# A two-layer decoder on one core: norms of three layers by other engines beside a recurrence, sums placed further behind their products, maxima of a tile in two instructions

## What is computed

```
x = LN(x + spectral(x))        # layer 0 "attention"
x = LN(x + cross0(x, ctx))     # 16 heads of 16, keys of length 154
...                            # a ternary FFN, then layer 1 with three more blocks

spectral(x):
    u = LN(x) @ W_to           # real and imaginary part, 64 frequencies each
    for t in range(1024):      # serial
        s = clip(rotate(decay * s + 0.1 * u[t]), -10, 10)
    y = x + 0.1 * (s @ W_from)                     # sum, then a norm ("L=1")
    return y + 0.1 * (gelu(LN(y) @ W1 + b1) @ W2 + b2)   # sum, then a norm ("L=2")
cross0: q, k, v, softmax(q k^T) v, Wo              # sum, then a norm ("L=3")
```

## Time and profile before

| what | value |
| --- | --- |
| median of three runs | 2186.43 us |
| profiled execution, its own time | 2188.24 us |
| its span | 2186.4 us |
| recurrence, first scan to last clip | 62.5 to 602.4 us |
| first stage behind it begins | about 692.6 us |
| VectorE busy over the span | 1429.5 us (65%) |
| TensorE busy over the span | 1782.3 us (82%) |
| ScalarE busy over the span | 960.6 us (44%) |
| GpSimd busy over the span | 497.6 us (23%) |

### The profile page before, as it was taken

One profiled execution on the slowest core, in us unless ns is written; L12 is line 12 of the kernel. 1 busy time (PEld: TensorE's weight loads), 2 busy tenths in 40 slices (PEclk: granted clock), 3 DMA queues, 4 the chain that ended last, 5 costly groups with the idle time before them and its releaser, 6 DMA issues.

```text
span 2186.4 us, 34562 instructions
## 1 busy us (share of the span) xinstructions
PE 1782.3 (82%) x12969; PEld 1277.3 (58%) x12969; DVE 1429.5 (65%) x4585; ACT 960.6 (44%) x2259; POOL 497.6 (23%) x602
## 2 busy tenths in 40 slices
PE   3547666766677877999999999999888999998808
PEld 1335455654564335666666766666657999884306
DVE  4888777787822586666666566666735666663695
ACT  3524333443344743444444345445314455543762
POOL 3011112111120022333333333333302333330002
PEclk9767788878787986999999999999989999999959
DMA  5000000000000011100000000000303333310001
GB/s 153 1 1 1 1 1 1 1 1 1 1 1 1 1 39 46 38 1 1 1 1 1 1 1 1 1 1 1 122 6 88 88 83 67 86 30 0 0 0 39
DMA packets 86311, 49.81 MB, mean 23 GB/s; under 512 B 40205, under 2 KB 83905, under 8 KB 85953
## 3 DMA queue, kind: packets, MB, share of 16 engines
q1 hardware_dynamic: 79361, 47.05, 8.3%
q10 hardware_dynamic: 6784, 0.56, 0.3%
HBM read 45.50 MB, written 2.10 MB: 22 GB/s over the span
## 4 chain that ended last, share of the span: by engine, by line
PE 61%; DVE 18%; ACT 10%; POOL 3%; issue 3%; POOLq 0%; DVEq 0%; ACTq 0%
PE PS L1525 7%; PE PS L1555 6%; PE PS L1822 6%; PE PS L1542 5%; PE PS L713 3%; PE PS L1510 3%; PE PS L1500 3%; DVE sq L667 3%; DVE nx L664 3%; PE PS L719 3%; PE PS L2235 3%; PE PS L1885 2%; PE PS L1570 2%; PE PS L1841 2%; PE PS L1850 2%
## 5 line engine op out<-in xcount | busy, mean ns | idle before, releaser
L1678 POOL TENSOR_SCALAR px<-px,crl 128x128 f32<-128x128 f32 (+7 forms) x128 | 222.7, 1740 | 429.9 <-DVE crl L1650 429.9
L1593 ACT ACTIVATE px<-PS,cnm 128x128 f32<-128x128 f32 (+7 forms) x256 | 187.6, 737 | 229.4 <-DVE cnm L1635 229.4
L1635 DVE TENSOR_REDUCE cnm<-PS 128x1 f32<-128x128 f32 (+7 forms) x256 | 181.8, 751 | 73.7 <-PE PS L1530 72.0
L182 POOL TENSOR_SCALAR rstd<-mv 128x1 f32<-128x1 f32 x128 | 41.6, 325 | 796.4 <-DVE mv L161 795.7
L667 DVE TENSOR_SCALAR sq<-nx 128x4 f32<-128x4 f32 x1024 | 184.9, 181 | 35.2 <-DVE nx L664 0.2
L664 DVE TENSOR_TENSOR_SCAN nx<-sq 128x6 f32<-128x6 f32 x1024 | 175.4, 171 | 35.5 <-SPq L2302 2.3
L1542 PE MATMUL PS<-ident,px 128*128 128x128 f32 x1152 | 160.0, 278 | 5.1 <-DVE pT L1643 2.3
L1525 PE MATMUL PS<-kT,qT 64*128 64x512 f32 (+3 forms) x768 | 158.6, 517 | 3.3 <-ACT px L1593 1.4
L1542 PEld LDWEIGHTS PS<-ident,px 128*128 128x128 f32 x1152 | 129.2, 141 | 53.9 <-issue 34.7
L1555 PE MATMUL PS<-pT,V 128*64 128x128 f32 x2304 | 153.8, 278 | 0.0
L1912 ACT ACTIVATE YT<-YT,xnm 128x154 f32<-128x154 f32 x256 | 104.8, 414 | 93.9 <-DVE xnm L1954 93.9
(11 more groups left out here) (317 smaller groups left out, 3781.9 us busy)
## 6 DMA issues: line engine op xcount, KB each, us to landing
xbs<-in_fside_Bx16xSxS SPq DMA_DIRECT2D x8, 1232.0 KB, 6.6
fsrc<-in_fside_Bx16xSxS SPq DMA_DIRECT2D x8, 1232.0 KB, 6.6
xmk<-in_mask_Bx16xSxS_bk SPq DMA_DIRECT2D x8, 308.0 KB, 8.6
fsrc<-in_mask_Bx16xSxS_bk SPq DMA_DIRECT2D x8, 308.0 KB, 8.2
X<-in_x SPq DMA_DIRECT2D x1, 2048.0 KB, 11.5
w<-in_L_attn_W_ffn SPq DMA_DIRECT2D x2, 1024.0 KB, 12.5
t<-in_L_ffn_w SPq DMA_DIRECT2D x2, 1024.0 KB, 11.3
out<-xs SPq DMA_DIRECT2D x16, 128.0 KB, 1.7
```

The source lines that it names most:

```text
L1593: e.activation(k.px[n % 2][:, h, 0:width], src, ACT.Exp, bias=k.cnm[:, n % 4, h:h + 1], accum_out=k.cl[:, n % 4, h:h + 1]).then_inc(sem("c ...
L1635: e.tensor_reduce(k.cnm[:, n % 4, h:h + 1], src, AX.X, ALU.max, negate=True).then_inc(sem("c.max"), 1)
L1678: e.tensor_scalar(k.px[n % 2][:, 0, 0:width], k.px[n % 2][:, 0, 0:width], k.crl[:, n % 4, 0:1], None, ALU.mult).then_inc(sem("c.normal0"), 1)
```

## The change

- `aside(L, T)` is true for L = 1, 2, 3 and all tiles but the last of each batch (t = 7). These norms leave VectorE: ScalarE makes the sum of a row (an activation with an accumulator), GpSimd the negative mean, ScalarE the sum of squares about it, GpSimd three instructions for the scale and the shift, and `side` on ScalarE is as it was. The last tiles take VectorE's `stats`, `aggr` and `unit` (a tensor_scalar) and no `shift` or `side`.
- In `network_chain` sum L=1 is placed 16 instead of 10 steps behind `from`, and sum L=2 22 instead of 14 behind the second `down`, for t < 6. The norm's own distances are 5 and 6 (squares, side) where they were 5 (side). For t = 7 all of a norm follows its sum at once.
- `top` is one instruction for each part. `score(T, 1)` waits for the whole of part 0.
- New: the tiles `ljunk` and `lst`, and a running count of what ScalarE and GpSimd have done of these norms (`k.ln_act`, `k.ln_pool`).

```diff
+def aside(L, T):
+    return L in (1, 2, 3) and T % BT < BT - 1
...
+    def mean(L, T):
+        s = k.lst[:, lane_of(L, T), :]
+        w.wait_ge("ln.act", k.ln_act["sum", L, T])
+        e.tensor_scalar(s[:, 1:2], s[:, 0:1], -1.0 / D, None, ALU.mult).then_inc(sem("ln.pool"), 1)
...
+        s, rs, n = k.lst[:, lane_of(L, T), :], k.rstd[:, lane_of(L, T), :], k.ln_pool["shift", L, T]
+        w.wait_ge("ln.act", k.ln_act["square", L, T])
+        e.tensor_scalar(rs[:, 0:1], s[:, 2:3], 1.0 / D, 1e-5, ALU.mult, ALU.add).then_inc(sem("ln.pool"), 1)
+        w.wait_ge("ln.pool", n - 2)
+        e.tensor_tensor(rs[:, 1:2], rs[:, 0:1], k.neghalf[:, :], ALU.pow).then_inc(sem("ln.pool"), 1)
+        w.wait_ge("ln.pool", n - 1)
+        e.tensor_tensor(s[:, 3:4], s[:, 1:2], rs[:, 1:2], ALU.mult).then_inc(sem("ln.pool"), 1)
...
+    def total(L, T):
+        n, lane = k.ln_act["sum", L, T], lane_of(L, T)
+        w.wait_ge("ln.r", at("r", L, T))
+        w.wait_ge("ln.act", n - 2)
+        e.activation(k.ljunk[:, n % 2, :], k.r4[:, lane, :], ACT.Identity, accum_out=k.lst[:, lane, 0:1]).then_inc(sem("ln.act"), 1)
+
+    def square(L, T):
+        n, lane = k.ln_act["square", L, T], lane_of(L, T)
+        w.wait_ge("ln.pool", k.ln_pool["mean", L, T])
+        w.wait_ge("ln.act", n - 2)
+        e.activation(k.ljunk[:, n % 2, :], k.r4[:, lane, :], ACT.Square, bias=k.lst[:, lane, 1:2], accum_out=k.lst[:, lane, 2:3]).then_inc(sem("ln.act"), 1)
...
     def norm(L, gap):
-        for kind, wait in (("r", gap), ("stats", 0), ("aggr", 0), ("shift", 0), ("side", 5), ("turn", 2), ("put", 0)):
+        beside = (("sum", 0), ("mean", 0), ("square", 5), ("shift", 0), ("side", 6), ("turn", 2))
+        alone = (("stats", 0), ("aggr", 0), ("unit", 0), ("turn", 0))
+        for kind, wait in (("r", gap), *(beside if t < BT - 1 else alone), ("put", 0)):
...
-    yield from norm(1, 10)
+    yield from norm(1, 16 if t < BT - 2 else 10)
...
-    yield from norm(2, 14)
+    yield from norm(2, 22 if t < BT - 2 else 14)
...
-    yield 1, ("stats", 3, T)
-    yield 1, ("aggr", 3, T)
-    yield 0, ("shift", 3, T)
-    yield 6, ("side", 3, T)
+    if aside(3, T):
+        yield 0, ("sum", 3, T)
+        yield 0, ("mean", 3, T)
+        yield 5, ("square", 3, T)
+        yield 0, ("shift", 3, T)
+        yield 6, ("side", 3, T)
+    else:
+        for kind in ("stats", "aggr", "unit"):
+            yield 0, (kind, 3, T)
...
-                    w.wait_ge("n.max", 8 * (n - 1) + j + 1)
+                    w.wait_ge("n.max", 2 * (n - 1) + 1)
...
-        for j in range(4):
-            if part:
-                dst, src = k.nnm[:, 3, j, 0:1], PS[:, 4 + j, 0:S2]
-            else:
-                dst, src = k.nnm[:, 0:3, j, 0], PS[:, 4 + j, 0:3 * S2].rearrange("p (m s) -> p m s", m=3)
-            e.tensor_reduce(dst, src, AX.X, ALU.max, negate=True).then_inc(sem("n.max"), 1)
+        if part:
+            dst, src = k.nnm[:, 3, :, 0], PS[:, 4:8, 0:S2]
+        else:
+            dst, src = k.nnm[:, 0:3, :, 0].rearrange("p m j -> p j m"), PS[:, 4:8, 0:3 * S2].rearrange("p j (m s) -> p j m s", m=3)
+        e.tensor_reduce(dst, src, AX.X, ALU.max, negate=True).then_inc(sem("n.max"), 1)
```

More of the change, by code:

```diff
@@ L165, in unit @@
         w.wait_ge("ln.rstd", at("aggr", L, T))
-        if L == 0:
+        if L in (0, 1):
             w.wait_ge("ln.turn", k.turn_before.get((L, T), 0))
@@ L169, in unit @@
             w.wait_ge(f"store{lane}", 16 * (T // LANES))
[L170 removed]
+        dst = k.xs4[:, lane, :] if L in (0, 1, 7) else k.xt(T)
         e.tensor_scalar(dst, src(L, T), k.mv[:, lane, 0:1], k.rstd[:, lane, 1:2], ALU.subtract, ALU.mult).then_inc(sem("ln.unit"), 1)
@@ L184, in aggr @@
         e.tensor_tensor(rs[:, 1:2], rs[:, 0:1], k.neghalf[:, :], ALU.pow).then_inc(sem("ln.rstd"), 1)
+    def mean(L, T):
+        s = k.lst[:, lane_of(L, T), :]
+        w.wait_ge("ln.act", k.ln_act["sum", L, T])
+        e.tensor_scalar(s[:, 1:2], s[:, 0:1], -1.0 / D, None, ALU.mult).then_inc(sem("ln.pool"), 1)
     def shift(L, T):
[L188 to L192, removed]
+        s, rs, n = k.lst[:, lane_of(L, T), :], k.rstd[:, lane_of(L, T), :], k.ln_pool["shift", L, T]
[5 more added lines that the diff above has]
+        e.tensor_tensor(s[:, 3:4], s[:, 1:2], rs[:, 1:2], ALU.mult).then_inc(sem("ln.pool"), 1)
+    return {"aggr": aggr, "mean": mean, "shift": shift}
 def norm_tensor(e, w, k):
@@ L199, in turn @@
         lane = lane_of(L, T)
-        if L in (1, 2):
+        if aside(L, T):
             w.wait_ge("ln.side", at("side", L, T))
@@ L216, in norm_scalar @@
     sem, at = k.sem, k.order.at
+    def total(L, T):
[8 more added lines that the diff above has]
+        e.activation(k.ljunk[:, n % 2, :], k.r4[:, lane, :], ACT.Square, bias=k.lst[:, lane, 1:2], accum_out=k.lst[:, lane, 2:3]).then_inc(sem("ln.act"), 1)
     def side(L, T):
         lane = lane_of(L, T)
-        w.wait_ge("ln.shift", at("shift", L, T))
+        w.wait_ge("ln.pool", k.ln_pool["shift", L, T])
         if L == 1:
@@ L223, in side @@
         dst = k.xs4[:, lane, :] if L == 1 else k.xt(T)
-        e.activation(dst, k.r4[:, lane, :], ACT.Identity, scale=k.rstd[:, lane, 1:2], bias=k.rstd[:, lane, 0:1]).then_inc(sem("ln.side"), 1)
+        e.activation(dst, k.r4[:, lane, :], ACT.Identity, scale=k.rstd[:, lane, 1:2], bias=k.lst[:, lane, 3:4]).then_inc(sem("ln.side"), 1)
     def put(L, T):
@@ L236, in put @@
         m.then_inc(sem("ln.put"), 1)
-    return {"side": side, "put": put}
+    return {"sum": total, "square": square, "side": side, "put": put}
 def flips_tensor(e, w, k):
@@ L822, in near_tiles @@
     k.ny = sb("ny", [P, D], scope=sc)
+    k.ljunk = sb("ljunk", [P, 2, D], BF16, scope=sc)
     k.nyT = sb("nyT", [P, DC, P], scope=sc)
@@ L897, in peak @@
         n = at("n.query", T)
-        w.wait_ge("n.max", 8 * n)
+        w.wait_ge("n.max", 2 * n)
         for m in range(4):
@@ L2361, in build @@
         k.rstd = sb("rstd", [P, LANES, 2])
+        k.lst = sb("lst", [P, LANES, 4])
         k.ctxT = sb("ctxT", [P, DC, B * S2])
@@ L2399, in build @@
         swiglu_order(k)
+        k.ln_act, k.ln_pool, acts, pools = {}, {}, 0, 0
+        for step in k.order.steps:
+            acts += step[0] in ("sum", "square")
+            pools += {"mean": 1, "shift": 3}.get(step[0], 0)
+            k.ln_act[step], k.ln_pool[step] = acts, pools
         k.turn_before, held = {}, {}
```

## The result

The changed kernel takes **2207.92 us** in the median of 4 runs (2206.95 to 2208.81), the kernel before 2186.54 (2186.07 to 2187.50). The ratio is **1.0096**, with a 95% interval of 1.0081 to 1.0111: slower by about 21 us. Its profiled execution took 2207.14 us, with a span of 2205.3, 18.9 more than before.

What follows compares the result with a forecast made beforehand. A closed loop of VectorE, TensorE and ScalarE bounds each chunk (70.0 us). Terms -4.8 (chunk 1), +6.5 (chunks 2 to 6), +8.1 (chunk 7), +3.9 (behind) sum to +13.7: 2200 us, forecast 2188 to 2212, range 2177 to 2214.

Steps and rivals of the forecast that it cites:

- new wait at second top b: VectorE at slot 49 waits 7.8 us for score b part 1, which stands behind up0 to up3 on TensorE.
- Peak a to queries b: From second top a's end until ScalarE ends queries b: 10.3 us, as in the kernel before.
- The norm: Norm L=1 on ScalarE and GpSimd, row sums through put: 7.6 us, no quicker than before (7.3), only starting later.
- What leaves VectorE: Per chunk 1.8 us of statistics, 0.4 for L=3 norms, 0.8 for maxima: 3.0 us, which vanish into waits.
- The maxima: Tops in one instruction a part on VectorE: 0.2 us saved each, 0.8 a chunk, 0.8 behind the recurrence.
- The first sums: Stretch totals inside the recurrence: chunk 1 -4.8 us, chunk 7 with its old gaps +8.1 us.
- Behind the recurrence: After the last scan: network sums about 4 and 6 us later, some given back by norms and maxima, in all +3.9.
- The ternary stage: The stage after the recurrence and what follows it: predicted to change by 0.
- The waits did not vanish: Rival 2: the norm's chain is off the loop and VectorE's waits vanish, -50 us, 2136; chance 0.09.
- TensorE at the quick pace: Rival 1: products between peak a and queries b, and up0, up1, run quicker; chunk 67.4, total 2177; chance 0.15.
- Square with a table load: Rival 3: each square on ScalarE loads a table, 6 x 1.28 us more, 2208; chance 0.07.
- Ups at the slow pace all the way to peak b: Ups on TensorE stay slow until peak b, 2222 us; the rival left, number 4, has chance 0.09.

Runs made afterwards that it cites:

- e11: The changed kernel with the maxima as before, in four instructions a part, score part 1 released bank by bank: 2207.7 us, ratio 1.0089.
- e1: The kernel before with only the shorter maxima, two instructions a tile: 2174.1 us, ratio 0.9933.
- e6: The changed kernel with the wide gaps of 16 and 22 steps in chunk 7 too: 2201.4 us, ratio 1.0061.
- e7: The changed kernel with the query of each a tile, and so cross attention, 34 steps later: 2176.1 us, ratio 0.9945.
- e5: The changed kernel with the first top 15 instead of 20 steps behind its score, one number: 2170.7 us, ratio 0.9925.
- e2: The kernel before with only the two gaps widened to 16 and 22 steps, norms on VectorE: 2209.9 us, ratio 1.0100.
- e3: The changed kernel with the old gaps of 10 and 14 steps in all chunks: 2221.1 us, ratio 1.0151.
- e12: The changed kernel with the norms of the last tiles (t = 7) on ScalarE and GpSimd too: 2208.7 us, ratio 1.0094.

## Why the prediction was right, and where its sum was off

The forecast was 2200 us, in a range of 2177 to 2214, slower with 0.68; measured 2207.9. The direction and the path were right; the size was +21.4 for +13.6. Its main step, that queries b ahead of the row sums on ScalarE start the norm late and that the wait comes back at the second top b, is what the rows show. Times into chunk 5 (which starts at 392.09):

| step | predicted | measured |
| --- | --- | --- |
| second top a ends | 6.9 | 6.9 |
| queries b end | 17.2 | 18.3 |
| up0 starts | 24.8 | 25.0 |
| VectorE is free for second top b | 25.8 | 27.1 |
| score b part 1 ends | 33.6 | 33.9 |
| new wait at second top b | 7.8 | 6.9 |
| sum L=2, and its wait | 52.2, 2.7 | 52.1, 2.1 |
| chunk | 71.3 | 71.8 |

- **Peak a to queries b** was taken over as 10.3 and took 11.4: the granted clock was 0.50 until 408 us, so query b took 2.95 us (2.05 in the kernel before, where the clock was back at 1.00 from 394).
- **The norm** was counted at 7.6 and took 6.8 (410.31 to 417.12). The two row sums and two squares with their reads took 1.96 (410.31 to 412.27), not 3.0, since they overlap; the product on GpSimd, bounded by 0.27 and 0.57, took 0.19. That the two errors, of queries b and of the norm, cancel to 0.2 at up0 is luck.
- **What leaves VectorE** was counted at 3.0 us a chunk, and its busy time fell by 1.8. Of the missing 1.2, 0.7 are the scan and the clip behind sum L=1 that are stretched by 0.9 while GpSimd adds (one scan was stretched by 0.2 before); the rest I didn't trace. The prediction had no such term. The 0.9 are also most of the 1.3 by which VectorE comes later to the second top b, so the new wait is 6.9 and not 7.8; as VectorE waits there anyway, the chunk is no longer for it.
- **The maxima** take 2.08 and 0.79, against 2.28 and 0.98: the 0.2 a part was right as busy time. That it would vanish into the waits of the loop, as the prediction had it, e11 bears out; the 0.8 counted for it behind the recurrence is not seen (96.6 with and without). At the places of the kernel before, which the prediction did not price, it gives 1.4 a chunk (e1, 69.9 to 68.5), and most of that is TensorE's pace at peak b.
- **The first sums** came out as said: chunk 1 -4.0 for -4.8, chunk 7 +7.4 for +8.1, and e6 shows that its old gaps are the cause of the latter.
- **Behind the recurrence** was the term most off, +6.0 for +3.9. VectorE after the last scan at 612.61:

```profile
625.87 0.76 DVE L710 SCALAR_TENSOR_TENSOR r<-PS,X 128x256 f32<-128x256 f32 x2 [12.88 <-PE PS L733]
...
629.66 0.81 DVE L176 TENSOR_SCALAR xs<-r,mv,rstd 128x256 f32<-128x256 f32 x1 [0.46 <-POOL rstd L189]
630.38 2.07 DVE L1058 TENSOR_REDUCE nnm<-PS 128x12 f32<-128x1848 f32 x1
...
660.90 0.76 DVE L710 SCALAR_TENSOR_TENSOR r<-PS,X 128x256 f32<-128x256 f32 x2 [9.11 <-PE PS L747]
```

Against the last scan the two sums stand at 13.3 and 48.3 us, before at 8.5 and 39.2: 4.8 and 9.1 later, where the prediction had 4 and 6. The maxima of b come behind the norm on VectorE (630.38), so peak b and its queries lie among the ups, which the working had only half counted. Behind the second sum 3.1 came back, where 2.1 were counted.
- **The ternary stage**, taken at nothing, was 2.0 us longer. The lists of work there are the same, and over all the kernels here it is between 184.2 and 188.1 us (185.4 before). The cause is open. e11, where only the maxima differ, has 185.4 us there against 187.5.
- The remaining 2.5 us lie between the spans (+18.9) and the medians (+21.4): the profiled execution of before was 1.7 above its median, that of after 0.8 below.

**The rivals.** The waits did not vanish (2136) in any order that was tried; e7, where the row sums don't stand behind queries b, came nearest with chunks of 63 to 65, against 61.4. TensorE at the quick pace (2177) did not come in the changed kernel, but in part in e5: turned a is quick, peak a is not, and queries b end 9.1 us behind the second top, for which 8.2 was worked out and 11.4 is what the changed kernel takes. Square with a table load (2208) would have given the measured 2207.9 almost to the tenth, so the time alone could not decide against it; the rows do. The groups of ScalarE, 62 to 720 us (busy us, mean ns):

```profile
L784 ACT ACT_TABLE_LOAD x14 | 18.0, 1283 | 0.2
L1018 ACT ACT_TABLE_LOAD x14 | 18.0, 1283 | 0.2
L242 ACT ACTIVATE ljunk<-r,lst 128x256 bf16<-128x256 f32 x42 | 21.0, 501 | 2.5 <-POOL lst L194 2.5
```

There are 14 loads ahead of the gelus and 14 ahead of the exponentials, as before, and none at L242. The Trainium skill (ScalarE: Activation LUTs, What ACT_TABLE_LOAD costs) gives 1283 ns for a load, which these rows show to the nanosecond, and a drain of some 1380 ns with it, which they don't: in chunk 5 an exponential ends at 433.97, the load runs from 433.99 to 435.27, and the gelu starts at 435.28. Ups at the slow pace all the way to peak b (2222) did not come either: the clock was 0.50 from up0 through mix a and 1.00 from 422 us on, and the pace cost what it did at query b.

What stays open: why TensorE takes its quick pace in one order and not in another. The rows show what it does, and the experiments changed it only by moving work. Over the whole execution the granted clock is 0.901 before, 0.887 to 0.898 in every kernel that is slower than it (after, e2, e3, e6, e11, e12), and 0.900 to 0.912 in the others. So no run tells the order of the work and TensorE's pace apart.

## What to carry to other kernels

Where each engine walks one fixed list, work that leaves the critical engine is only free if it is not listed behind something later on its new engine: look at what stands ahead of it there before counting what it saves. A gap in such a list moves everything that hangs on it, so ask what each number drags along; here one number, five steps of a maximum, was worth 37 us, with all that it moved and TensorE's pace, more than the 21 that the change lost. Parts that interact can't be priced one at a time, and a saving is worth its size only on the loop that bounds, more if other work on the loop gets shorter with it, little if a wait follows anyway. And look at what the work that you remove was covering: the statistics stood where GpSimd adds, and the step that took their place was stretched.

## What the runs showed of the hardware

- An accumulating activation brings one more instruction: 42 row sums have 42 ACTIVATION_READ_ACCUMULATOR of 195 ns, against 0.43 us for the row sum itself, and its start overlaps the end of the activation (387.83 + 0.43, the read from 388.14 in e5). The next row sum starts 0.40 us behind the first (388.23), so most of the read is hidden.
- A scan and a clip of 0.17 us took 0.58 to 0.66 and 0.65 while GpSimd added 128 x 256 tiles, once a chunk, in the kernel after and in e5; BATCH_NORM_STATS2 at the same time, in the kernel before, took its usual 0.74 for two.
- A small GpSimd product (128 x 1) takes 0.19 us and a power 0.57.
- A maximum of 4 x 462 elements in one instruction is 2.08 us, four of 462 together 2.28: an estimate from these is that merging saves about 70 ns an instruction (0.20 / 3), and from the short ones 60 (0.98 to 0.79).
- Products gated bank by bank held TensorE for 2.51 us in the kernel before; the same eight behind one wait took 1.37 + 0.68 = 2.05 in e1.
- TensorE's pace differs from place to place: the same eight products of peak took 1.05, 1.91 or 2.07 us. The granted clock of short windows goes with it: in the kernel after it was 0.94 as query b ended and 0.50 again at up0; from 410 to 416 TensorE was busy for 2.07 of 6 us. The windows, with the columns as above:

```profile
408.00:410.00 2.00, 1.26 (x10) 1.07 (x9) 1.66 (x10) 0.70 (x3) 0.00 (x0) 0.94 0.00 0
410.00:412.00 2.00, 1.07 (x24) 0.84 (x24) 1.69 (x10) 2.00 (x9) 0.57 (x3) 1.00 0.00 0
412.00:416.00 4.00, 1.00 (x4) 0.40 (x4) 3.62 (x13) 2.00 (x6) 3.59 (x9) 0.88 0.00 0
416.00:418.00 2.00, 0.88 (x2) 0.82 (x3) 1.80 (x7) 1.98 (x4) 0.22 (x1) 0.50 0.00 0
```
